# Expert stages: last expert's dot product copied once and the clamped candidates compared in one operation behind the first weighing, the product taken in the silu

## The reference, cut to what matters

```
q = W_q h            -> scores of 64 x-keys and 64 y-keys in each of 4 heads, top 8 of each
all_scores = sx + sy (64 pairs),  all_idx = ix * 64 + iy;  top 8 of the pairs per head
de = down_embed[indices];  ue = up_embed[indices]          # 1024 experts
w = silu((h . de) * softmax(scores))
out = silu(h W_up) W_down + sum over heads and picks of w * ue
```

## Time and profile before

| | |
|---|---|
| median of 3 runs | 3882.25 us |
| lowest and highest of them | 3873.7 and 3883.93 us |
| the profiled execution, its own time | 3882.03 us |
| its span in the trace | 3880.2 us |
| expert stages in the span | about 0 to 1045 us and 2130 to 3180 us |
| busy share of the span | PE 95%, DVE 84%, ACT 71%, POOL 64% |

### The profile page before, as it was taken

How to read it: one execution, slowest core, us unless ns; L and a number is a source line. 1 busy time by engine, 2 the same in 40 slices (tenths; PEclk the granted TensorE clock), 3 DMA queues, 4 the chain that set the end, 5 groups by cost and what they waited for, 6 DMA issues and landing times. The chain is left out here.

```text
span 3880.2 us, 79090 instructions
## 1 busy us (share of the span) xinstructions
PE 3669.8 (95%) x27416; PEld 3180.0 (82%) x27416; DVE 3241.5 (84%) x7734; ACT 2740.4 (71%) x7878; POOL 2466.3 (64%) x2334
## 2 busy tenths in 40 slices
PE   6999999999789999999998699999999969999989
PEld 5888888888668888888887588888888858898878
DVE  7999999999568888888876799999999958756577
ACT  6777777776379999999996577777777737532166
POOL 7778888777365555555551788888788737411365
PEclk9999999999899999999999899999999989999999
DMA  4556555565500000000000456565566552421442
GB/s 118 121 120 121 119 120 119 121 120 114 116 12 13 24 13 24 13 24 13 24 7 13 119 119 122 121 124 118 117 122 123 115 115 84 130 90 56 144 137 93
DMA packets 190350, 343.12 MB, mean 88 GB/s; under 512 B 14816, under 2 KB 138112, under 8 KB 189952
## 3 DMA queue, kind: packets, MB, share of 16 engines
q0 software_dynamic: 55296, 201.35, 27.3%
q1 hardware_dynamic: 134656, 136.71, 11.1%
HBM read 80.06 MB, written 56.62 MB: 35 GB/s over the span
## 5 line engine op out<-in xcount | busy, mean ns | idle before, releaser
L302 POOL TENSOR_TENSOR f_grid<-f_ex 128x1024 f32<-128x1024 f32 x512 | 1161.8, 2307 | 7.6 <-ACT f_ex L557 7.1
L1546 ACT ACTIVATE a_ex<-a_p_s,a_mneg 128x128 f32<-128x128 f32 x2048 | 728.1, 409 | 87.1 <-DVE a_mneg L1600 87.1
L717 DVE SCALAR_TENSOR_TENSOR f_p_u<-f_grid,f_te,f_p_dot 128x1024 f32<-128x1024 f32 x512 | 653.2, 1276 | 42.7 <-PE f_p_dot L106 42.4
L726 DVE SCALAR_TENSOR_TENSOR f_q<-f_p_u,f_rz,f_grid 128x1024 f32<-128x1024 f32 x512 | 652.5, 1274 | 11.4 <-PE f_p_wT L446 6.8
L312 POOL DMA_DIRECT2D f_q<-f_q x384 | 385.5, 1005 | 389.0 <-DMA f_q<-f_q 249.2
L1546 ACT ACTIVATION_READ_ACCUMULATOR a_ex<-a_p_s,a_mneg 128x1 f32 x2048 | 507.9, 248 | 0.0
L458 PE MATMUL f_p_y<-f_wdn,f_hs 128*128 128x256 f32 x2048 | 489.5, 382 | 1.3
L463 PE MATMUL f_p_y<-f_eup,f_wT 128*128 128x256 f32 x2048 | 473.1, 379 | 0.0
L463 PEld LDWEIGHTS f_p_y<-f_eup,f_wT 128*128 128x128 f32 x2048 | 380.2, 190 | 46.5
L458 PEld LDWEIGHTS f_p_y<-f_wdn,f_hs 128*128 128x128 f32 x2048 | 372.3, 192 | 44.7 <-issue 3.6
L1600 DVE TENSOR_REDUCE a_mneg<-a_p_s 128x4 f32<-128x512 f32 x512 | 335.4, 676 | 6.0 <-PE a_p_s L1400 6.0
(11 more groups left out here) (645 smaller groups left out, 11072.3 us busy)
## 6 DMA issues: line engine op xcount, KB each, us to landing
f_q<-f_q POOLq DMA_DIRECT2D x384, 512.0 KB, 4.8
x_f<-f_yt SPq DMA_DIRECT2D x64, 256.0 KB, 2.2
f_xt<-x SPq DMA_DIRECT2D x32, 256.0 KB, 3.3
a_xt<-x_f SPq DMA_DIRECT2D x16, 512.0 KB, 3.8
x_a<-a_yt SPq DMA_DIRECT2D x16, 512.0 KB, 3.0
f_xt<-x_a SPq DMA_DIRECT2D x32, 256.0 KB, 3.1
c_xt<-x_f SPq DMA_DIRECT2D x16, 512.0 KB, 4.6
x_c<-c_yt SPq DMA_DIRECT2D x16, 512.0 KB, 3.1
```

Of the source, the lines that this page charges most:

```text
L302: g_grid.mark(pool.tensor_tensor(grid[v][:, hd, :].rearrange("p (i j) -> p i j", i=XROWS), sx[:, hd, :].unsqueeze(2).to_broadcast([P, XROW ...
L717: d_mask.mark(dve.scalar_tensor_tensor(out=p_u[:], in0=grid[v][:, hd, :], scalar=te[:, v, hd, TOP - 1:TOP], in1=p_dot[:], op0=ALU.is_ge, o ...
L726: d_mul.mark(dve.scalar_tensor_tensor(out=q[v][:, hd, :], in0=p_u[:], scalar=rz[:, v, hd:hd + 1], in1=grid[v][:, hd, :], op0=ALU.mult, op1 ...
L1546: last = act.activation(ex[t.step % 2][:, i, n, :], p_s[i][:, n, :], ACT.Exp, bias=mneg[:, i, n:n + 1], accum_out=z[t.step % 2][:, i, n:n ...
```

## The change

`tail_dots` no longer multiplies. It copies the column of expert 1023 from `p_dot` to a new tile `dot` (one instruction, 1 element per partition) and compares all four heads' clamped picks with their limits in one instruction of 32 elements, so that `u8` is 0 or 1. ScalarE's silu takes `dot` as its scale, which is where the product is now made. `tail_dots` moves from between the fourth mask and the fourth weighing to behind the first weighing of the same tile. The marks of `d_mask` are put in the new order, and `dots` waits for the fourth mask rather than for `tail`.

```diff
-        d_mask = m.track("d_mask", *(k for v in range(V) for k in (*parts[HEADS * v:HEADS * (v + 1)], f"{v}tail")))
+        d_mask = m.track("d_mask", *(k for v in range(V) for k in (f"{v}0", f"{v}tail", *(f"{v}{hd}" for hd in range(1, HEADS)))))
...
                     if v:
-                        d_mask.wait(pe, t, "0tail")
+                        d_mask.wait(pe, t, f"0{HEADS - 1}")
                     elif (t - 1).exists():
-                        d_mask.wait(pe, t - 1, "1tail")
+                        d_mask.wait(pe, t - 1, f"1{HEADS - 1}")
...
-                    a_silu.mark(act.activation(w8[:, v], u8[:, v], ACT.Silu, accum_out=clamped[:, v:v + 1]), f"tail{v}")
+                    a_silu.mark(act.activation(w8[:, v], u8[:, v], ACT.Silu, scale=dot[:, v:v + 1], accum_out=clamped[:, v:v + 1]), f"tail{v}")
...
-                    for hd in range(HEADS):
-                        last = dve.scalar_tensor_tensor(
-                            out=u8[:, v, hd, :], in0=te[:, v, hd, TOP:], scalar=te[:, v, hd, TOP - 1:TOP],
-                            in1=p_dot[:, EXPERTS - 1:EXPERTS].to_broadcast([P, TOP]), op0=ALU.is_ge, op1=ALU.mult)
-                    d_mask.mark(last, f"{v}tail")
+                    dve.tensor_copy(dot[:, v:v + 1], p_dot[:, EXPERTS - 1:EXPERTS])
+                    d_mask.mark(dve.tensor_tensor(u8[:, v], te[:, v, :, TOP:],
+                                                  te[:, v, :, TOP - 1:TOP].to_broadcast([P, HEADS, TOP]), ALU.is_ge), f"{v}tail")
...
                         mask(t, v, 0)
                         weigh(t, v, 0)
+                        tail_dots(t, v)
                         if after:
                             maxes(t + 1, v, range(0, 3))
...
                         mask(t, v, 3)
-                        tail_dots(t, v)
                         weigh(t, v, 3)
```

More of the change, by code:

```diff
@@ L197, in expert_ffn @@
         z, rz = (m.sbuf(k, V, HEADS) for k in ("z", "rz"))
-        clamped = m.sbuf("clamped", V)
+        clamped, dot = m.sbuf("clamped", V), m.sbuf("dot", V)
         grid = [m.sbuf(f"grid{v}", HEADS, EXPERTS) for v in range(V)]
```

## The result

| | before | changed |
|---|---|---|
| median | 3883.09 us (4 runs) | 3931.88 us (4 runs) |
| lowest to highest | 3873.7 to 3884.38 | 3926.17 to 3935.19 |
| span of the profiled execution | 3880.2 us | 3933.4 us |

The ratio is 1.0134, with a 95% interval of 1.012 to 1.0148. The change costs 49 us, or 0.76 us in each of 64 turns if all of it falls there; the mean turn in the two traces grew by 0.75 us. The forecast of 3884 us was wrong, and so was its range.

The account below looks back on a forecast made before the run. The prediction took a closed loop of ScalarE, GpSimd and its accumulating DMAs as the bound. 3 us passing minus 0.7 us at `dots` gave 2.3 us on 3882.03 us: 3884 us, range 3862 to 3902 us.

Parts of the forecast that it names:

- Added on VectorE: Copy from PSUM plus 32-element comparison in each tile: 0.22 us together, between 0.16 and 0.27.
- What bounds the kernel now: Expert stages: a closed loop of ScalarE, GpSimd and its accumulating DMAs sets the pace, 30.91 us a turn on average.
- the ring: Loop from ScalarE's clamped-picks silu through `front`, GpSimd's DMA issues and list to the next silu; 29.90 us in one turn.
- Removed on VectorE: The four small instructions of each tile go away: 0.54 us per tile, 0.135 us each.
- the lost cover: Fourth weighing now directly follows the fourth mask it reads: 1.32 us instead of 1.18, so 0.14 us come back.
- The scale: ScalarE's clamped-picks silu takes a per-partition scale: about 0.08 us longer, 5.0 us in all if everything passes.
- The output and the store: Tile 1's output and store come later against GpSimd's DMA, lengthening its transfer: 0.15 us per turn, 9.3 us if all passes.
- quick and slow turns: Turns said to alternate: store 1.25 us ahead of the accumulating DMA, transfer 5.22 us; or 0.25 us ahead, 6.37 us.
- the store meets the DMA: Rival, chance 0.15: with 1.03 us of lead the first transfer is as slow as with 0.25; 3896 us, up to 3910.
- Ceiling of the lead: Largest time by which the store is issued ahead of the accumulating DMA: 1.25 us now, 1.03 after the change.
- What passes: Share of additions per turn reaching the total, the DMA giving most back: +3 us of a possible 14.3.
- The sum: +3 us for additions that pass, -0.7 us for the shorter wait of `dots`: 2.3 us on 3882.03, so 3884 us.

Follow-up runs that it names:

- Cutting the ring: Kernel before, tile 0's four old instructions behind the first weighing and GpSimd's clamped-picks multiply directly behind tails(t, 0): 3868.92 us, ratio 0.9973.
- the pointer alone: Kernel before, only the clamped picks' silu reading its scale from a tile of ones: 3881.14 us against 3876.92, ratio 1.0009.
- the moved four: Kernel before, the four old instructions of each tile moved behind the first weighing, dots waiting for the fourth mask: 3909.44 us, ratio 1.0075.
- the kernel with the pair in its pauses: Changed kernel, copy and comparison behind the second weighing in tile 0, behind the first in tile 1: 3883.2 us, ratio 1.0006.

## Why the prediction was wrong, point by point

- **The step that failed** is "Added on VectorE". It bounded the pair by 0.16 and 0.27 us and took 0.22. In tile 1 it costs 0.17 us from copy to MAX8 (531.96 to 532.13). In tile 0 the comparison alone is shown with 1.27 us on average, (93.1 - 64 x 0.18) / 64. The bounds came from instructions with one input in PSUM and from MAX8, none of which is held; the comparison is of another kind, and the rows were near in size, not in kind.
- **The trace of before did have a row of that kind**, outside the expert stages. The channel mix has an instruction of VectorE with both inputs in SBUF. These are its durations, and those of another of the same size with one input in PSUM:

```profile
L1115 DVE TENSOR_TENSOR c_yt<-c_rk,c_xt x32: 1224/1667/2641, 3223.1 to 3875.6; 128x1024 f32<-128x1024 f32 x32
```

```profile
L1103 DVE TENSOR_TENSOR c_ks<-c_relu,c_p_k x32: 1203/1222/1222, 3208.2 to 3865.7; 128x1024 f32<-128x1024 f32 x32
```

 Two times 128x1024, the one with 1.20 to 1.22 us every time, the other between 1.22 and 2.64. The longest of the first kind began while a GpSimd instruction was running:

```profile
3223.13 2.64 DVE L1115 TENSOR_TENSOR c_yt<-c_rk,c_xt 128x1024 f32<-128x1024 f32 x1
```

```profile
3222.29 2.39 POOL L902 TENSOR_TENSOR c_xr0l<-c_xr,c_xr0h 128x1024 fp32r<-128x1024 f32 x1
```

 The spread of a duration whose work is fixed is the sign of a hold. The Trainium skill has the rule: "GPSIMD Engine Reference", section "Specifications", says that GpSimd's SBUF interfaces are shared with VectorE, with contention for instructions that have two SBUF inputs or run in a two-port mode. The runs agree, 0.177 us with one input in PSUM against up to 2.62 us, and they show the contention to be a hold until GpSimd's pause. I did not weigh this rule, and it would have been the rival that came true.
- **What bounds the kernel now** was right: the ring closes in every turn, in the changed kernel too, and the prediction's sign against it (a wait of the ring gone from turns) did not appear. What it left out is how close the next loop lies. Cutting the ring gave 8 us, where the run's own expectation had 20 to 35: a second loop of about 30.4 to 30.6 us, from first mask by output and dense part to the next `p_dot`, lay right behind it. The prediction saw its row and gave it a chance as a gain only, while a hold inside it is a loss.
- **Removed on VectorE**, 0.54 us, and the lost cover, 0.14 us, were right: in the changed kernel fourth mask and fourth weighing start at 523.03 and 524.35, 1.32 us apart:

```profile
523.03 1.28 DVE L717 SCALAR_TENSOR_TENSOR f_p_u<-f_grid,f_te,f_p_dot 128x1024 f32<-128x1024 f32 x1
524.35 1.28 DVE L726 SCALAR_TENSOR_TENSOR f_q<-f_p_u,f_rz,f_grid 128x1024 f32<-128x1024 f32 x1
```

 The rule of the Trainium skill that the prediction quotes (VectorE: DVE Perf Modes, "The DRAIN you can't avoid"), that a semaphore costs nothing extra between two chained operations, is not borne out here either: 1.32 us against 1.18.
- **The scale**: 0.08 us predicted; the instruction went from 0.23 to 0.31 us, the ring's piece from 8.65 to 8.77, and to 8.75 with the pointer alone. Mis-sized by 0.02 to 0.04 us.
- **The output and the store**: the road was right, and most of the loss came by it, since the hold made the output late and the first transfer took 0.59 us more. The slope was right for means only: 1.15 predicted, about 1 between the kernel before and the moved four, but at one and the same lead of 1.25 us single turns took 5.21 and 6.19 us. That the transfer is fixed by the lead, from which the prediction reads its quick and slow turns, is not borne out. Its sign for the rival "the store meets the DMA", a transfer above 6.2 us with a lead near 1.0, stood in the trace of before already (store at 309.29, lead 0.99 us, transfer 6.97 us), so it could not have told anything. Ceiling of the lead 1.03 predicted for an unheld pair, 1.18 in the kernel with the pair in its pauses. The pair takes 0.17 us from it, not 0.22, and the pointer gives 0.10 us to it, since it delays the ring's DMA and not the store (the ceiling with the pointer alone is 1.35). The prediction had left the second out.
- **What passes**: "an addition is given back" holds for small ones only. For the move of the four, 0.54 us ahead of the output cost 0.37 us per turn. That small ones are given back is compatible with the runs (2.3 us for the pair in its pauses, 4.2 us for the pointer alone), but with intervals of some 7 us it is not shown.
- **The sum**, +2.3 us, is met by the kernel with the same instructions and hardly any hold, +2.3 us against its own kernel before. That it is met so closely is luck: the interval is -1 to +6 us, tile 0's pair stands elsewhere there, and the terms for pair, scale and ceiling were each off by some hundredths that partly cancel. One term, the hold, was missing, and it carried the miss.

## What to carry to other kernels

Before adding a small instruction of VectorE that reads only SBUF, look at what GpSimd does at that very time: it may cost 0.18 us or several us, and the time stands inside the instruction, with no wait in front of it. Keep one input in PSUM if there is one, or put it where GpSimd is seen to wait for something, and check both tiles of an unrolled loop. When the rows near a new operation differ from it in where they read, search the whole trace for one that reads as it does and look at the spread of its durations, not at the mean.

## What the runs showed of the hardware

- A VectorE comparison of 32 elements with both inputs in SBUF took 0.18 us while GpSimd paused and up to 2.65 us beside it in the changed kernel (4.08 us with the pair behind the second weighing); with one input in PSUM 0.175 to 0.179 us in all 128 cases.
- The hold lasts over several GpSimd instructions in a row: 3.42 us over two grid products, ending 0.06 us from their end. It also began at 513.73, while GpSimd's row showed a DMA issue, 0.17 us before the product.
- A VectorE instruction with a single streamed input, from SBUF to SBUF with a per-partition scalar, was held too (up to 2.85 us, 8 elements). The MAX8, which read SBUF alone, were not held (0.153 to 0.236 us for the three shapes of 16 to 64 elements), nor was the copy from PSUM (0.145 to 0.149 us).
- It goes the other way too. In the channel mix of the kernel before, GpSimd's instruction of 4 elements took 0.23 us by itself and 1.21 us when VectorE's instruction with both inputs in SBUF had started 0.10 us before it:

```profile
3204.41 0.23 POOL L135 TENSOR_SCALAR c_ve<-c_mv 128x4 f32<-128x4 f32 x1
...
3234.05 1.21 POOL L135 TENSOR_SCALAR c_ve<-c_mv 128x4 f32<-128x4 f32 x1
```

```profile
3233.95 1.23 DVE L1115 TENSOR_TENSOR c_yt<-c_rk,c_xt 128x1024 f32<-128x1024 f32 x1
```

- An accumulating DMA of 512 KB inside SBUF took 5.1 us from issue to next issue in most turns where it was the ring's second (5.10 us at 544.44), and up to 7.98 us where it was the first and a 256 KB store was issued 0.12 us behind it (store at 411.58 in the changed kernel), with a 256 KB load 0.4 us behind the store.
